# Embedding bags on one core: twenty features counted and twelve gathered, with gathers that wait on TensorE's count

## The chip, the cores and the metric

The kernel runs on one core of a Trainium2 chip. The metric is the device time of one execution in microseconds (us), taken as the median of several runs. The program uses all five engines: TensorE (PE in the rows, PEld for its weight loads), VectorE (DVE), ScalarE (ACT), GpSimd (POOL) and SyncE (SP), the last of which only issues DMAs here. A trailing q (SPq) means an engine's sequencer.

## The reference, cut to what matters

There are 512 samples, 32 features, up to 20 lookups a bag, tables of 12500 rows and 64 numbers a row. A bag's result is the sum of the first `length` rows that its ids name.

```python
flat = tables.reshape(F_ * V_, E_)
offs = jnp.arange(F_, dtype=ids.dtype)[None, :, None] * V_
emb = flat[ids + offs]
mask = (jnp.arange(L_) < lengths[..., None]).astype(emb.dtype)
pooled = jnp.einsum('bfle,bfl->bfe', emb, mask)
out = pooled.reshape(Bq, F_ * E_)
return jnp.nan_to_num(out)
```

## The kernel before, in words

The features are split in two kinds, which are worked on side by side.

**Counted features** (the first M = 22). For such a feature the whole table is loaded, and TensorE multiplies it by a matrix that says how often each bag names each row. The order is written out by hand. A feature has two halves of 256 samples, each of 7 chunks, which makes 14 *stages* a feature, numbered 0 to 13 here. In a stage VectorE makes the one-hot operands: one `onehot_p` (L740) and six `onehot_j` (L742). TensorE multiplies these into `pairs` (L515, in `count`), three evictions a stage. One more eviction stands at the head of each half (`single`, L726 and L728), so a feature has 44. ScalarE copies each from PSUM into `counts` (L470, in `save_counts`). Between the pairs TensorE multiplies the counts of the half before by the table (`sums`, L525). The semaphore `counted` rises by one with each eviction that TensorE has written. VectorE may begin stage s once stage s-2 has been counted (`AHEAD = 2`), so it can run almost two stages ahead of TensorE. In stages 6, 9 and 12 VectorE also splits a piece of the table into bfloat16 parts (`cut_rest` L751, `cut_low` L759). In stages 1 and 8 it reads the sums (L778), and in stage 10 it cleans the result (`clean_pooled`). SP loads the next table chunk in stages 0 to 6 and stores the feature before in stage 11.

**Gathered features** (the other 10). Their 5120 bags are sorted by length and cut into 40 *tiles* of 128 bags. A tile's rows are fetched with one indirect DMA a lookup (L427, in `gather`): lookup l of 128 bags at once, as many as its longest bag has. GpSimd issues them. There are 8 buffers, so the tiles run in 5 *bodies* of 8. In each body deep and shallow tiles take turns (`sorted_tile`). VectorE adds a tile's rows with one reduction (L800, in `add_rows`) and cleans four tiles after every fourth. GpSimd then puts these four with four indirect DMAs (L437, in `put`). After an add, SP clears the buffer with zeros (L346) and loads the next records (L350). The adds stand at the end of stages 0, 4 and 13 of even features and 3 and 11 of odd ones, from feature 2, stage 13 on (`ADDS`, `FIRST_ADD`).

The gather of lookup l waits for the landing of the last gather but one of its tile. So at most two gathers of a tile are in flight. TensorE's and GpSimd's programs are loops; VectorE's, ScalarE's and SP's are written out in full. Feature 0 also holds the preparation: VectorE sorts the lengths and works out the columns of the lookups between its first stages (`prepare`).

Of the kernel before, what the change touches and what calls it, by code (L numbers as in the profile page):

```python
# [22 lines left out]

P = 128
M = 22
TRIO = 3
GROUP = 2 * TRIO
SETS = 2
# [11 lines left out]
def turn(l):  # L40
    return l % 2
# [5 lines left out]

PARTED_BY_VECTOR = {6: 1, 9: 3, 12: 6}

ADDS = (0, 4, 13), (3, 11)  # L50
FIRST_ADD = 2, 8
READ_FIRST, READ_SECOND, CLEAN = 1, CHUNKS + 1, CHUNKS + 3

SKIP = 1 << 22
# [8 lines left out]
ALU = mybir.AluOpType  # L63
# [6 lines left out]
I32 = mybir.dt.int32  # L70
# [11 lines left out]
def build_embedding_bag(nc, ids, lengths, tables, lookup_ids, lookup_lengths, lookup_place, ramps, triangle,  # L82
                        out_counted, out_gathered):
    B, F, L = ids.shape
    _, V, E = tables.shape
    J, HALF, GROUPS = geometry(B, V)
    G = F - M
    BLOCKS = B // P
    TILES = BLOCKS * G
# [5 lines left out]
    CE = JC * E  # L95
    HALVES = M * 2
    N = HALVES * GROUPS
# [6 lines left out]
    BODIES = TILES // BUFFERS  # L104
    STAGES = 2 * CHUNKS
# [10 lines left out]
    STORES = 2 * TRIO + LAST_WORDS  # L116


    added_at = {}
    for f in range(M):  # L120
        for stage in ADDS[f % 2]:
            if (f, stage) >= FIRST_ADD and len(added_at) < TILES:
                added_at[f, stage] = len(added_at)
    LEFT = len(added_at)

    with ExitStack() as ctx:
        def sb(name, shape, dt):
            return ctx.enter_context(nc.sbuf_tensor(name, shape, dt))
# [31 lines left out]
        place_now = sb("place_now", [P, BUFFERS], I32)  # L160
        rank = sb("rank", [P, TILES], I32)
        depth = sb("depth", [P, TILES], I32)

        arrived, arrival = (sb(name, [P, 2, TILES], I32) for name in ("arrived", "arrival"))
        is_nan = sb("is_nan", [P, max(BLOCKS, SLOTS) * E], U8)

        FIRST_HALVES = slice(0, 2)
# [31 lines left out]
        rank_f, depth_f = piece(TILES, F32), piece(TILES, F32)  # L199

        runs_f = until[:, 4 * TILES:(4 + L // 4) * TILES].rearrange("p (t q) -> p t q", t=TILES)
        turn_f, arrival_f = (until[:, 2 * x * TILES:2 * (x + 1) * TILES].rearrange("p (x t) -> p x t", x=2) for x in range(2))
# [28 lines left out]
        counted = sem("counted")  # L231
# [17 lines left out]
        rows_in = [[sem(f"rows_in{k}_{x}") for x in range(2)] for k in range(BUFFERS)]  # L249
# [55 lines left out]
        def column(t):  # L305
            return t % BUFFERS * BODIES + t // BUFFERS
# [7 lines left out]
        def _(sp):  # L314
# [54 lines left out]

            for f in range(1, M):  # L370
                for stage in range(STAGES):
# [11 lines left out]
        @block.gpsimd  # L383
        def _(pool):
            for out, pattern, base, by in (
                (value, [[1, L + 1]], 0, 0),
                (first_row, [[V, G], [0, L]], M * V, 0),
                (position, [[0, G], [1, L]], 0, 0),
                (records[:, :, L], [[P, TILES]], 0, 1),
                (lane[:], [[1, 1]], 0, 1),  # L390
            ) + tuple(
                (last_rank[:, column(k):column(k) + BODIES],
                 [[(sorted_tile(k + BUFFERS) - sorted_tile(k)) * P, BODIES]], sorted_tile(k) * P + P - 1, 0)
                for k in range(BUFFERS)
            ):
                nc.gpsimd.iota(out, pattern=pattern, base=base, channel_multiplier=by).then_inc(iotas_done, 1)
            last_row = pool.to_reg(F * V - 1)

            for k in range(BLOCKS):
                pool.wait_ge(records_ready, k + 1)  # L400
                for t in range(k * G, (k + 1) * G):
                    nc.gpsimd.indirect_dma_start(  # L402
                        out=sorted_records, out_offset=bass.IndirectOffsetOnAxis(ap=rank[:, t:t + 1], axis=0),
                        in_=records[:, t, :], in_offset=None).then_inc(records_out, 16)
            pool.wait_ge(records_out, 16 * TILES)
            for t in range(BUFFERS):
                s = sorted_tile(t)
                nc.gpsimd.dma_start(row_now[:, t, :], sorted_records[s * P:(s + 1) * P, :]).then_inc(first_records_in, 16)
            pool.wait_ge(depths_ready, 1)
            pool.wait_ge(first_records_in, 16 * BUFFERS)  # L410

            def gather(b, k):

                pool.wait_ge(buffer_ready[k], b * 32 + 16)
                pool.sem_inc(fill_begun, 1)
                n = pool.value_load(depth[0:1, bass.ds(b + column(k), 1)], min_val=2, max_val=L)
                landed = [pool.value_load(arrived[0:1, x, bass.ds(b + column(k), 1)], min_val=0, max_val=16 * L * BODIES)
                          for x in range(2)]
                with ExitStack() as deeper:
                    for l in range(L):  # L420
                        if l > 1:
                            deeper.enter_context(pool.If(n > l))
                        x = turn(l)
                        if l > 1:
                            pool.wait_ge(rows_in[k][x], landed[x] + 16 * sum(turn(i) == x for i in range(l)))
                            pool.sem_inc(fill_begun, 1)
                        nc.gpsimd.indirect_dma_start(  # L427
                            out=rows[:, k, l * E:(l + 1) * E], out_offset=None, in_=table_rows,
                            in_offset=bass.IndirectOffsetOnAxis(ap=row_now[:, k, l:l + 1], axis=0),
                            bounds_check=last_row, oob_is_err=False).then_inc(rows_in[k][x], 16)  # L430

            def put(b, x):

                pool.wait_ge(gathered_ready, b * 2 + (x + 1))
                pool.sem_inc(fill_begun, 1)
                for k in range(x * SLOTS, (x + 1) * SLOTS):
                    nc.gpsimd.indirect_dma_start(  # L437
                        out=out_gathered, out_offset=bass.IndirectOffsetOnAxis(ap=place_now[:, k:k + 1], axis=0),
                        in_=gathered[:, k * E:(k + 1) * E], in_offset=None).then_inc(gathered_stored[x], 16)

            def body(b, first):
                for k in range(BUFFERS):
                    if not first and k % SLOTS == PUT_AT:
                        put(b - 1, k // SLOTS)
                    gather(b, k)

            body(0, True)
            with pool.Fori(1, BODIES) as b:
                body(b, False)
            for x in range(2):  # L450
                put(BODIES - 1, x)
                pool.wait_ge(gathered_stored[x], 16 * SLOTS * BODIES)
# [148 lines left out]
        def _(dve):  # L601
            done = [0]

            def step(ins):
                done[0] += 1
                ins.then_inc(prepared, 1)
                dve.wait_ge(prepared, done[0])
# [42 lines left out]
            def find_depths():  # L650

                fits = has[:, 0:TILES * L].rearrange("p (t l) -> p t l", l=L)
                step(nc.vector.tensor_tensor(fits, below[:, 1:L + 1].unsqueeze(1).to_broadcast([P, TILES, L]),
                                             last_rank.unsqueeze(2).to_broadcast([P, TILES, L]), ALU.is_le))
                step(nc.vector.tensor_reduce(out=depth_f, in_=fits, axis=AX_X, op=ALU.add))
                step(nc.vector.tensor_reduce(out=runs_f, in_=fits.rearrange("p t (q x) -> p t q x", x=4)[:, :, :, 1::2],
                                             axis=AX_X, op=ALU.add))
                step(nc.vector.tensor_reduce(out=turn_f[:, 1, :], in_=runs_f, axis=AX_X, op=ALU.add))
                step(nc.vector.tensor_scalar(depth_f, depth_f, 2.0, None, ALU.max))
                step(nc.vector.tensor_scalar(turn_f[:, 1, :], turn_f[:, 1, :], 1.0, None, ALU.max))  # L660
                step(nc.vector.tensor_copy(depth[:], depth_f))
                step(nc.vector.tensor_tensor(turn_f[:, 0, :], depth_f, turn_f[:, 1, :], ALU.subtract))
                for k in range(BUFFERS):
                    mine = slice(column(k), column(k) + BODIES)
                    for x in range(2):
                        nc.vector.tensor_tensor_scan(arrival_f[:, x, mine], turn_f[:, x, mine], turn_f[:, x, mine], 0.0,
                                                     ALU.add, ALU.max).then_inc(scanned, 1)
                dve.wait_ge(scanned, 2 * BUFFERS)
                step(nc.vector.tensor_tensor(turn_f, arrival_f, turn_f, ALU.subtract))
                step(nc.vector.tensor_scalar(arrived[:], turn_f, 16.0, None, ALU.mult))  # L670
                step(nc.vector.tensor_scalar(arrival[:], arrival_f, 16.0, None, ALU.mult))
                dve.sem_inc(depths_ready, 1)

# [226 lines left out]
```

## Time and profile before

| what | us |
|---|---|
| median of 3 runs | 1185.06 |
| lowest and highest run | 1184.69, 1189.72 |
| span of the profiled execution | 1287.7 |
| TensorE busy in it | 1118.5 |
| VectorE busy in it | 992.5 |
| GpSimd busy in it | 547.5 |

The profiled execution is 102.6 us longer than the median of the runs shown. Its span is from the first to the last instruction; no separate total of it is given. Feature f begins for VectorE at 9.2, 92.6, 143.7 us and so on; features 16 to 21 begin at 960.1, 1012.8, 1060.1, 1109.8, 1158.7 and 1207.8 us. The last gather is issued at 958.2 us and the last add at 1074.7 us, so features 19 and 20 hold counted work alone.

### The profile page before, as it was taken

What the parts mean: (1) busy time and instruction counts of PE and PEld (TensorE: products, weight loads), DVE (VectorE), ACT (ScalarE), POOL (GpSimd) and SP (SyncE); (2) the same over time, 40 slices, a digit from 0 to 9 for tenths busy, and PEclk for the clock granted to TensorE, in tenths of its full rate; (3) what the DMA queues carried; (4) which work ended last, traced back from release to release, by engine and by line L of the source; (5) the groups of instructions that cost most, each with busy time, mean ns of one, the idle gap of its engine ahead of it and who ended that gap; (6) DMA issues with size and microseconds to landing.
All of it is one profiled execution on the core that took longest, in us unless ns stands there. A gap on an engine that the chain in (4) does not pass through costs nothing.

```text
span 1287.7 us, 31751 instructions
## 1 busy us (share of the span) xinstructions
PE 1118.5 (87%) x10873; PEld 969.4 (75%) x10873; DVE 992.5 (77%) x2692; ACT 827.6 (64%) x1233; POOL 547.5 (43%) x519
## 2 busy tenths in 40 slices
PE   3379999896988878989979888979789999999996
PEld 1168888785876767778868767868678888888886
DVE  9657788884886867869868867969678898787881
ACT  4257787673756656757747566757557777787780
POOL 4865665556555455555565544555540101000000
PEclk9989999897999988999989989989989999999998
DMA  5324234241433333242414333242413213123120
GB/s 184 116 68 115 60 83 144 74 136 45 135 107 95 117 86 97 81 132 82 143 46 136 106 95 118 82 130 69 134 25 100 58 55 104 47 62 100 35 73 5
DMA packets 63916, 118.38 MB, mean 92 GB/s; under 512 B 30120, under 2 KB 31742, under 8 KB 63840
## 3 DMA queue, kind: packets, MB, share of 16 engines
q1 hardware_dynamic: 46608, 102.19, 25.5%
q0 software_dynamic: 16032, 15.00, 5.9%
q10 hardware_dynamic: 1200, 0.50, 0.2%
q14 instruction: 68, 0.56, 0.1%
q8 instruction: 8, 0.13, 0.0%
HBM read 87.19 MB, written 4.62 MB: 71 GB/s over the span
## 4 chain that ended last, share of the span: by engine, by line
PE 73%; DVE 10%; another core or an unknown queue 7%; ACT 7%; issue 3%; DVEq 0%; POOL 0%; POOLq 0%
PE sums L525 48%; PE pairs L515 19%; PE rest L543 6%; DVE onehot_j L742 3%; ACT counts L470 3%; ACT table L482 2%; DVE gathered L800 1%; DVE onehot_p L740 1%; ACT rest L478 1%; DVE table L751 1%; ACT table L486 0%; DVE table L759 0%; DVEq L796 0%; DVE is_nan L768 0%
## 5 line engine op out<-in xcount | busy, mean ns | idle before, releaser
L525 PE MATMUL sums<-table,counts 128*128 128x192 bf16 x8624 | 909.0, 251 | 0.8 <-issue 0.8
L470 ACT ACTIVATE counts<-pairs 128x588 int16<-128x588 f32 (+1 forms) x968 | 617.0, 650 | 368.9 <-PE pairs L515 262.7
L525 PEld LDWEIGHTS sums<-table,counts 128*128 128x128 fp8e3 x8624 | 776.3, 98 | 55.0 <-issue 0.4
L427 POOL DMA_INDIRECT rows<-tables,row_now x413 | 453.3, 1098 | 376.7 <-issue 206.1
L742 DVE TENSOR_SCALAR onehot_j<-ramp,j_of,worth 128x296 bf16<-128x296 f16 x1848 | 536.3, 353 | 0.0
L515 PE MATMUL pairs<-onehot_j,onehot_p 128*128 128x294 bf16 x1892 | 410.4, 297 | 112.8 <-ACT counts L470 67.3
L740 DVE TENSOR_TENSOR onehot_p<-ramp,p_of 128x768 bf16<-128x768 f16 x308 | 169.9, 552 | 253.7 <-PE pairs L515 172.9
L515 PEld LDWEIGHTS pairs<-onehot_j,onehot_p 128*128 128x128 bf16 x1892 | 178.2, 98 | 187.3 <-issue 107.8
L543 PE MATMUL rest<-table,minus_eye 128*128 128x448 bf16 x352 | 102.5, 373 | 38.2 <-ACT table L482 17.1
L486 ACT ACTIVATE table<-rest 128x896 f32<-128x896 f32 x88 | 80.8, 918 | 35.3 <-remote 23.6
L437 POOL DMA_INDIRECT out_gathered<-gathered,place_now x40 | 42.4, 1061 | 132.3 <-DVE gathered L771 121.0
L482 ACT ACTIVATE table<-rest 128x896 f32<-128x896 f32 x88 | 80.8, 918 | 26.1 <-remote 9.8
L800 DVE TENSOR_REDUCE gathered<-rows 128x64 f32<-128x1280 f32 x40 | 94.3, 2356 | 0.0
L478 ACT ACTIVATE rest<-table 128x896 f32<-128x896 f32 x88 | 80.7, 917 | 0.0
L751 DVE TENSOR_TENSOR table<-table 128x896 f32<-128x896 f32 x66 | 71.5, 1083 | 0.0
L759 DVE TENSOR_TENSOR table<-table 128x896 f32<-128x896 f32 x66 | 69.5, 1053 | 0.0
L543 PEld LDWEIGHTS rest<-table,minus_eye 128*128 128x128 bf16 x352 | 24.2, 98 | 58.4 <-ACT table L482 25.6
L402 POOL DMA_INDIRECT sorted_records<-records,rank x40 | 45.6, 1139 | 26.3 <-DVE records L617 14.4
L778 DVE TENSOR_REDUCE pooled<-sums 128x128 f32<-128x384 f32 x44 | 23.8, 542 | 21.3 <-PE sums L525 20.5
L728 DVE TENSOR_SCALAR onehot_j<-ramp,j_of,worth 128x296 bf16<-128x296 f16 x44 | 17.3, 392 | 0.0
L726 DVE TENSOR_SCALAR onehot_p<-ramp,p_of 128x128 bf16<-128x128 f16 x44 | 12.8, 291 | 0.0
L771 DVE COPY_PREDICATED pooled<-is_nan,zeros 128x256 f32<-128x256 uint8 x22 | 10.0, 453 | 0.8
(68 smaller groups left out, 79.8 us busy)
## 6 DMA issues: line engine op xcount, KB each, us to landing
table<-tables SPq DMA_DIRECT2D x154, 448.0 KB
rows<-zeros SPq DMA_DIRECT2D x40, 640.0 KB
rows<-tables,row_now POOLq DMA_INDIRECT x413
out_counted<-pooled SPq DMA_DIRECT2D x132, 21.0 KB
rows<-lookup_ids SPq DMA_DIRECT2D x1, 903.0 KB, 8.5
rows<-lookup_lengths SPq DMA_DIRECT2D x1, 903.0 KB, 10.2
out_counted<-pooled SPq DMA_DIRECT2D x44, 1.0 KB
sorted_records<-records,rank POOLq DMA_INDIRECT x40
```

The lines of the kernel that those rows point to most:

```text
L427: nc.gpsimd.indirect_dma_start(out=rows[:, k, l * E:(l + 1) * E], out_offset=None, in_=table_rows, in_offset=bass.IndirectOffsetOnAxis(ap= ...
L470: nc.scalar.activation(dst, src, ACT.Copy).then_inc(counts_saved, 1)
L478: nc.scalar.activation(rest[:, :, 0:CE // 2], both_halves(0, c), ACT.Copy).then_inc(chunk_copied, 1)
L482: nc.scalar.activation(both_halves(1, c), rest[:, :, 0:CE // 2], ACT.Copy).then_inc(middle_ready, 1)
L486: nc.scalar.activation(both_halves(2, c), rest[:, :, 0:CE // 2], ACT.Copy).then_inc(low_saved, 1)
L515: last = nc.tensor.matmul(pair(h, c, q)[:, x, 0:WIDE], onehot_p[:, s, k, :, side], onehot_j[:, s, i + 1, 0:WIDE], start=True, stop=True)
L525: last = nc.tensor.matmul(sums[h][:, k * PARTS * E:(k + 1) * PARTS * E], counts[h][:, j, :, k], parts[:, :, j, :, 1], start=(j == 0 and k ...
L543: last = nc.tensor.matmul(rest[:, x, 0:CE // 2], minus_eye[:], upper_halves(part)[:, half], start=False, stop=True, skip_group_check=True)
L740: nc.vector.tensor_tensor(onehot_p[:, s, 1:, :, :], ramp_twice.unsqueeze(1).to_broadcast([P, PAIRS, P, 2]), of_chunk.unsqueeze(2).to_broad ...
L742: nc.vector.tensor_scalar(onehot_j[:, s, i + 1, :], ramp[:, 2 * P:], j_of[:, n:n + 1], worth[:, 0:1], ALU.is_equal, ALU.mult).then_inc(one ...
L751: nc.vector.tensor_tensor(table[:, 1, sl], table[:, 0, sl], upper_halves(0)[:, sl], ALU.subtract).then_inc(rest_done, 1)
L800: nc.vector.tensor_reduce(out=gathered[:, k * E:(k + 1) * E], in_=rows[:, k, :].rearrange("p (l e) -> p e l", e=E), axis=AX_X, op=ALU.add)
```

## The change

M goes from 22 to 20. So two features fewer are counted, and twelve are gathered: 48 tiles in 6 bodies in place of 40 in 5. The adds stand at stage number 41 + 5t for tile t (number 14 f + stage of the whole run), which is feature 2, stage 13 for the first and feature 19, stage 10 for the last. The gathers no longer wait for landings. Before lookups 0, 2, 4, ... GpSimd waits until `counted` has reached a value that depends on the tile and the lookup: 72 evictions for the first tile, 31 more for each pair of tiles, 125 more for each body, 7 more for each five lookups. An odd tile begins later by an amount from its depth (`later`, one more VectorE instruction in the preparation), and `arrived` goes, with two VectorE instructions.

```diff
-M = 22
+M = 20
...
-ADDS = (0, 4, 13), (3, 11)
-FIRST_ADD = 2, 8
+FIRST_ADD = 41
+ADD_EVERY = 5
+FIRST_GATHER = 72
+PAIR_OF_TILES = 31
+PER_BODY = 125
+
+def since(l):
+    return 7 * l // 5
...
+    added_at = {divmod(FIRST_ADD + ADD_EVERY * t, STAGES): t for t in range(TILES)}
...
-                landed = [pool.value_load(arrived[0:1, x, bass.ds(b + column(k), 1)], min_val=0, max_val=16 * L * BODIES)
-                          for x in range(2)]
+                start = b * PER_BODY + (FIRST_GATHER + PAIR_OF_TILES * (k // 2))
+                if k % 2:
+                    start = start + pool.value_load(later[0:1, bass.ds(b + column(k), 1)], min_val=0, max_val=PAIR_OF_TILES)
...
-                        x = turn(l)
-                        if l > 1:
-                            pool.wait_ge(rows_in[k][x], landed[x] + 16 * sum(turn(i) == x for i in range(l)))
+                        if l % 2 == 0:
+                            pool.wait_ge(counted, start + since(l))
                             pool.sem_inc(fill_begun, 1)
...
+                nc.vector.tensor_scalar(later[:], depth_f, -1.4, PAIR_OF_TILES - 2.0, ALU.mult, ALU.add)
...
-                step(nc.vector.tensor_tensor(turn_f, arrival_f, turn_f, ALU.subtract))
-                step(nc.vector.tensor_scalar(arrived[:], turn_f, 16.0, None, ALU.mult))
```

On GpSimd, in the first gathers of the first tile, before:

```order
L427 DMA rows<-tables,row_now 128x64 x2
L422 COMPARE_AND_BRANCH
L425 REGISTER_ALU
L427 DMA rows<-tables,row_now 128x64 [waits rows_in0_0]
L422 COMPARE_AND_BRANCH
L425 REGISTER_ALU
L427 DMA rows<-tables,row_now 128x64 [waits rows_in0_1]
```

On GpSimd, the head of the second tile (an odd one), after:

```order
L421 TENSOR_LOAD depth [waits buffer_ready1]
L421 ISA x2
L424 TENSOR_LOAD later
L424 ISA x2
L430 REGISTER_ALU
L432 DMA rows<-tables,row_now 128x64 [waits counted]
L432 DMA rows<-tables,row_now 128x64
L428 COMPARE_AND_BRANCH
L430 REGISTER_ALU
L432 DMA rows<-tables,row_now 128x64 [waits counted]
L428 COMPARE_AND_BRANCH
L432 DMA rows<-tables,row_now 128x64
```

Each gather from the third on waited for a landing (`rows_in`). Now each second gather waits for TensorE's count, the first of a tile too, and the one behind it waits for nothing.

On VectorE, from stage 12 of feature 6 on, before:

```order
L740 TENSOR_TENSOR onehot_p<-ramp,p_of 128x768
L742 TENSOR_SCALAR onehot_j<-ramp,j_of,worth 128x296 x2
L751 TENSOR_TENSOR table<-table 128x896
L742 TENSOR_SCALAR onehot_j<-ramp,j_of,worth 128x296 x3
L759 TENSOR_TENSOR table<-table 128x896
L742 TENSOR_SCALAR onehot_j<-ramp,j_of,worth 128x296
L740 TENSOR_TENSOR onehot_p<-ramp,p_of 128x768
L742 TENSOR_SCALAR onehot_j<-ramp,j_of,worth 128x296 x6
```

The same place on VectorE, from the second cut of the table on, after:

```order
L763 TENSOR_TENSOR table<-table 128x896
L746 TENSOR_SCALAR onehot_j<-ramp,j_of,worth 128x296
L800 TENSOR_LOAD arrival
L800 ISA x2
L800 TENSOR_LOAD arrival
L800 ISA x2
L804 TENSOR_REDUCE gathered<-rows 128x64
L807 COPY place_now<-row_now 128x1
L772 TENSOR_TENSOR is_nan<-gathered 128x256
L773 TENSOR_SCALAR gathered<-gathered 128x256
L775 COPY_PREDICATED gathered<-is_nan,zeros 128x256
L744 TENSOR_TENSOR onehot_p<-ramp,p_of 128x768
```

An add with its cleaning now stands behind the cuts of stage 12, ahead of the one-hots of stage 13. Before, no add stood in a stage that has cuts.

## Rows read from the trace of the kernel before

**Rows 1.** The page: span, and each engine's busy time.

```profile
span 1287.7 us, 31751 instructions
PE 1118.5 (87%) x10873; PEld 969.4 (75%) x10873; DVE 992.5 (77%) x2692; ACT 827.6 (64%) x1233; POOL 547.5 (43%) x519
```

**Rows 2.** The page's 40 slices: GpSimd busy, granted TensorE clock, both in tenths.

```profile
POOL 4865665556555455555565544555540101000000
PEclk9989999897999988999989989989989999999998
```

**Rows 3.** The page: shares of the chain of work that ended last.

```profile
PE 73%; DVE 10%; another core or an unknown queue 7%; ACT 7%; issue 3%; DVEq 0%; POOL 0%; POOLq 0%
```

**Rows 4.** Stretches: start:end length, each engine's busy us (instructions), clock, DMA.

```profile
0.00:92.60 92.60, 44.75 (x266) 27.01 (x267) 66.69 (x184) 36.76 (x54) 57.23 (x71) 0.94 0.37 127
92.60:143.70 51.10, 48.74 (x497) 43.17 (x496) 39.22 (x116) 37.65 (x57) 28.90 (x25) 1.00 0.31 82
92.60:960.10 867.50, 761.70 (x7409) 663.35 (x7408) 672.09 (x1802) 562.52 (x841) 481.33 (x440) 0.95 0.35 99
960.10:1109.80 149.70, 146.25 (x1489) 129.60 (x1487) 134.77 (x363) 113.12 (x169) 8.94 (x8) 1.00 0.24 69
1109.80:1158.70 48.90, 48.32 (x496) 43.10 (x494) 38.91 (x115) 37.55 (x57) 0.00 (x0) 1.00 0.25 69
1158.70:1207.80 49.10, 48.48 (x497) 43.21 (x496) 39.02 (x116) 37.71 (x57) 0.00 (x0) 1.00 0.23 68
1207.80:1287.70 79.90, 68.95 (x730) 63.13 (x727) 41.02 (x119) 39.91 (x60) 0.00 (x0) 0.95 0.15 44
```

**Rows 5.** Groups in feature 19 (1109.8 to 1158.7): busy, mean ns, idle before.

```profile
L525 PE MATMUL sums<-table,counts 128*128 128x192 bf16 x394 | 40.8, 247 | 0.0
L740 DVE TENSOR_TENSOR onehot_p<-ramp,p_of 128x768 bf16<-128x768 f16 x14 | 7.8, 555 | 9.9 <-PE pairs L515 9.9
```

**Rows 6.** Timeline of VectorE, an add in stage 13: start, length, engine, line.

```profile
1008.91 2.37 DVE L800 TENSOR_REDUCE gathered<-rows 128x64 f32<-128x1280 f32 x1
1011.37 0.42 DVE L768 TENSOR_TENSOR is_nan<-gathered 128x256 uint8<-128x256 f32 x1
...
1012.38 0.30 DVE L726 TENSOR_SCALAR onehot_p<-ramp,p_of 128x128 bf16<-128x128 f16 x1
```

**Rows 7.** Timelines: the first stage of all, then stages 12 and 13 of feature 19.

```profile
9.23 0.55 DVE L740 TENSOR_TENSOR onehot_p<-ramp,p_of 128x768 bf16<-128x768 f16 x1
10.93 0.66 ACT L470 ACTIVATE counts<-pairs 128x588 int16<-128x588 f32 x1 [0.76 <-PE pairs L515]
...
1156.19 0.54 DVE L740 TENSOR_TENSOR onehot_p<-ramp,p_of 128x768 bf16<-128x768 f16 x1
1159.50 0.67 ACT L470 ACTIVATE counts<-pairs 128x588 int16<-128x588 f32 x1 [0.42 <-PE pairs L515]
```

**Rows 8.** Line L427, all gathers: shortest, median and longest in ns.

```profile
L427 POOL DMA_INDIRECT rows<-tables,row_now x413: 991/1000/2072, 84.3 to 958.2; - x138
```

**Rows 9.** Timeline around 296 us, all engines; idle time before in brackets.

```profile
294.89 1.03 POOL L437 DMA_INDIRECT out_gathered<-gathered,place_now  x1 [0.30 <-issue]
295.42 1.39 SPq L342 DMA_DIRECT2D out_counted<-pooled  x2
...
304.39 0.66 ACT L470 ACTIVATE counts<-pairs 128x588 int16<-128x588 f32 x1 [8.97 <-remote]
```

**Rows 10.** Timelines of VectorE and GpSimd in the preparation.

```profile
12.66 1.03 DVE L645 TENSOR_TENSOR counts<-counts 128x840 f32<-128x840 f32 x1
...
44.78 0.96 POOL L402 DMA_INDIRECT sorted_records<-records,rank  x1 [0.30 <-issue]
...
47.99 2.03 DVE L681 SCALAR_TENSOR_TENSOR rows<-rows 128x1806 f32<-128x1806 f32 x1
...
48.50 2.84 POOL L402 DMA_INDIRECT sorted_records<-records,rank  x1 [0.30 <-issue]
```

More of the change, by code:

```diff
@@ L116, in build_embedding_bag @@
     STORES = 2 * TRIO + LAST_WORDS
[L119 to L124, printed above, removed]
+    added_at = {divmod(FIRST_ADD + ADD_EVERY * t, STAGES): t for t in range(TILES)}
+    assert FIRST_ADD + ADD_EVERY * (TILES - 1) < M * STAGES
+    LEFT = TILES
     with ExitStack() as ctx:
@@ L162, in build_embedding_bag @@
         depth = sb("depth", [P, TILES], I32)
-        arrived, arrival = (sb(name, [P, 2, TILES], I32) for name in ("arrived", "arrival"))
+        later = sb("later", [P, TILES], I32)
+        arrival = sb("arrival", [P, 2, TILES], I32)
         is_nan = sb("is_nan", [P, max(BLOCKS, SLOTS) * E], U8)
@@ L429, in gather @@
                             in_offset=bass.IndirectOffsetOnAxis(ap=row_now[:, k, l:l + 1], axis=0),
-                            bounds_check=last_row, oob_is_err=False).then_inc(rows_in[k][x], 16)
+                            bounds_check=last_row, oob_is_err=False).then_inc(rows_in[k][turn(l)], 16)
             def put(b, x):
```

## Prediction

> **What bounds the kernel now.** I read the page's busy times and slices first, then the chain of waits, then a table of stretches cut at the features, and last the timelines of single stages. TensorE is busiest, with 1118.5 of 1287.7 us, ahead of VectorE with 992.5 [rows 1], and it holds 73% of the chain that ended last [rows 3]. Averages hide what matters, so look at the stretches. Features 19 and 20 hold counted work alone. They take 48.9 and 49.1 us, and TensorE is busy for 48.3 and 48.5 us of that [rows 4]. A feature without gathers is TensorE's own work and nothing else; I take 49.0 us. In such a feature VectorE idles 9.9 us, all of it in waits for TensorE ahead of a stage's one-hots [rows 5]. This idle time is what the adds of gathered tiles live on.
>
> Features 1 to 15 have gathers, and in the profiled execution they take 867.5 us, or 57.8 us each [rows 4]. The clock is granted at 0.95 there and dips below full in several slices; GpSimd works through just these slices [rows 2, 4]. Now set this against the timed runs. The stretches at both ends are 92.6 us and 149.7 + 48.9 + 49.1 + 79.9 = 327.6 us [rows 4]. If the timed run matches the profile there, the fifteen features have 1185.06 - 92.6 - 327.6 = 764.9 us, or 51.0 us each. So the 102.6 us by which the profile exceeds the median lie almost wholly in the gather features. They come as single stalls: at 295.4 us, beside a put and a store, ScalarE stops for 8.97 us and the rest stops behind it [rows 9]. I treat such stalls as mostly the profiled execution's own and work against the median, keeping them as a rival.
>
> **The change part by part.**
>
> *Two counted features fewer.* They leave from the steady part: 2 x 49.0 = -98.0 us. Nothing hides this, as TensorE is the bound there [rows 4].
>
> *Preparation.* VectorE sorts 48 tiles in place of 40, so its instructions over all tiles grow by a fifth; one of 840 numbers takes 1.03 us [rows 10]. About ten of that size come to 10 x 0.2 = +2 us. The long ones over all lookups, such as that of 2.03 us [rows 10], shrink by a tenth, about -0.8 us. Two small instructions go and one comes. GpSimd sends 8 more tiles of sorted records at 0.96 + 0.30 = 1.26 us [rows 10], 10 us more. These are hidden: the gathers now begin at eviction 72, which is 28 evictions of 49.0 / 44 = 1.11 us behind 92.6 us, about 124 us, against 84.3 before [rows 8]. Sum: between 0 and +4, taken as +1.5 us.
>
> *The adds.* One add is 2.37 us, and every fourth has about 1.1 us of cleaning behind it: from 1008.91 to 1012.38 it is 3.47 us [rows 6]. Eight more come. What do they cost TensorE? Features 16 to 18 hold 7 adds and no gathers, and take 149.7 us where three bare features take 147.0: 2.7 us, or 0.39 us an add [rows 4]. Eight more at that rate are +3 us. Their new places cost more. VectorE begins stage 13's one-hots at 1156.19, and ScalarE takes the first eviction of that stage at 1159.50, a lead of 3.31 us; in the very first stage, where nothing is ahead, the same distance is 1.70 us [rows 7]. So the slack is 1.6 us. An add in stage 12 (3 of the 48, and two of these with cleaning) overdraws it by 2.37 - 1.6 = 0.8 or 3.47 - 1.6 = 1.9 us, together 4.6 us. Before, no add stood there. A walk through the other stages in the same way finds about 3 us more, in stages behind an add in stage 6 or 10 or with cleaning in stage 11, and 1 us that the old places cost. So the places add about +7 us, and all adds together +10. The bounds are +3 (the measured rate alone) and +22 (every add late by 0.8 us, 48 x 0.8 - 40 x 0.39).
>
> *More gathers.* 413 gathers for 40 tiles [rows 8] make about 496 for 48. Their cost to TensorE without adds shows in feature 1: 51.1 us against 49.0 with 25 of them [rows 4], 0.08 us each. By the median it is 764.9 - 15 x 49.0 = 30 us, less 13 us for the 33 adds there, over 408 gathers: 0.04 us each. 83 more at 0.06 are +5 us; bounds +3 and +7.
>
> *The new waits on TensorE's count.* Behind GpSimd's wait stand its own later gathers and the puts, and nobody else. The tile is waited for by VectorE's add. Tile 0 begins at eviction 72 and is issued by about 98, in stage number 31; its add stands at 41. Both advance by 10 stages a pair (31 evictions of 22/7 a stage are 9.9), so some nine stages of 3.5 us, 31 us, stay between them to the end. Is GpSimd fast enough? A pair has 413 / 40 x 2 = 20.7 gathers of 1.00 + 0.30 us [rows 8, 10], 26.9 us; two puts, 2.6 us; and two tile heads, about 2 us: 31.5 us. The pace is 31 evictions of about 51.7 / 44 = 1.17 us, 36.4 us. It keeps up, so the wait itself costs nothing. That gathers come evenly and never in bursts may also give something back: from 0 down to the whole price of gathers, 496 x 0.04 = -20 us. I take 0, as feature 1 paid its 2.1 us with gathers that were paced by landings. SP's new order, refills at other stages, costs nothing: it waits for an add that VectorE makes about a stage ahead of TensorE.
>
> *A rule that speaks against it.* While VectorE ran the 2.03 us instruction in the preparation, a GpSimd DMA that otherwise took 0.96 us took 2.84 us [rows 10]. The Trainium skill's page SBUF — State Buffer, section Who interferes with whom, has a VectorE instruction in a 2-port mode and GpSimd block each other fully. The row agrees. By that rule gathers could lengthen with more VectorE work; but the median gather is 1.00 us beside 49-us features full of VectorE work [rows 8], so the sum leaves it out and the slow rival below takes it up.
>
> **Sum.** 1185.06 - 98.0 + 1.5 + 10 + 5 = 1103.6; I say 1103 us. As a check by stretches: 94.1 for the head, 49.7 for feature 1, 17 features of 51.0 + 0.6, and 81 for the last, are 1102 us.
>
> **The rivals.**
>
> *Even pacing pays.* The gather features lose most of their extra: 1103 less 9 to 20 us, 1083 to 1094. For it: the bursts of puts, stores and gathers at the stall [rows 9]. Against it: puts and stores remain as they are.
>
> *VectorE becomes the bound.* The adds cost their upper bound, +22 in place of +10, perhaps a little more: 1113 to 1130. For it: VectorE's idle 9.9 us [rows 5] against 2.8 adds of 2.37 + 0.3 = 7.5 us a feature, unevenly placed.
>
> *The wait is empty.* If GpSimd is always late, `counted` has passed each value when it comes, and gathers run back to back as before but without landing waits. Nothing waits for them, so the time is the sum's, 1103 to 1110.
>
> *Stalls of the profiled kind stand in timed runs too.* Then a share of 9 us [rows 9] at each of 12 puts, say a third to two thirds of 108 us, comes on top: 1135 to 1175.
>
> *GpSimd falls behind and VectorE waits for rows (slower).* At x us a gather a pair takes 20.7x + 4.6 us against 36.4. The 31 us of slack are used up over 24 pairs once x is 1.6. Beyond, each pair adds its excess, and the run is slower than before when 24 (20.7x - 31.8) - 31 passes 82 us, at x = 1.76. With 1.8 us it is 1103 + 24 x 5.5 - 31 = 1204 us. Against it: the median is 1.30 with issue, and the longest of all is 2.07 [rows 8].
>
> **How the numbers follow.** Forecast (1094 to 1113) 0.46; pacing pays 0.22; VectorE the bound 0.18; wait empty 0.07; stalls 0.05; GpSimd behind 0.02. The range 1086 to 1124 takes the forecast, the empty wait and most of the two neighbours. A measurement of this kernel can tell about 0.5%, 6 us. Only the last case is slower and none lies near no change: faster 0.97, same 0.01, slower 0.02.
>
> **What would show it.** In the profile after: bare features of 49.0 us at its start only, since gathers reach feature 18; GpSimd's idle time before L432 released by TensorE in place of landings, in pairs of gathers about 3.3 us apart; in feature 6, stage 13 late by some 2 us behind the add of stage 12; a sum of adds of 48 x 2.37. Idle VectorE ahead of the adds' reduction would mean that GpSimd is behind. If gather features run near 49 us, the landing waits' bursts were the cost. I am wrong below 1086 if the extra of the gather features was not the adds' and gathers' at all, and above 1124 if the stalls belong to the timed runs.

## The result, and the profile after

The kernel after takes 1047.36 us (median of 4 runs, 1046.27 to 1047.80) against 1187.39 us for the kernel before in the same comparison (1184.69 to 1192.81). The ratio is 0.881, with a 95% interval of 0.878 to 0.885. The gain is 140 us where I had forecast 82, and the time lies 39 us below the range.

The page of the kernel after, in the lines that answer to [rows 1 to 3]:

```profile
span 1045.4 us, 29010 instructions
PE 983.3 (94%) x9885; PEld 864.1 (83%) x9885; DVE 937.4 (90%) x2485; ACT 754.1 (72%) x1121; POOL 666.0 (64%) x617
...
POOL 3874677676676756777667767767676775773010
PEclk9999999999999999999999999999999999999998
...
PE 79%; DVE 16%; ACT 2%; issue 1%; DVEq 1%; POOL 0%; POOLq 0%
```

The span is 2.0 us under the time of the same execution (1047.35 us). TensorE is busy for 94% of it in place of 87%, and its clock is granted at nine tenths or more in every slice but the last. Now the stretches, with the columns of [rows 4]: the head, feature 1, features 1 to 18, and the last feature with the tail.

```profile
0.00:74.20 74.20, 40.86 (x266) 25.10 (x266) 67.09 (x183) 36.26 (x54) 46.43 (x57) 1.00 0.43 154
74.20:123.20 49.00, 48.42 (x497) 43.17 (x496) 39.30 (x115) 37.64 (x57) 24.93 (x28) 1.00 0.30 79
74.20:965.10 890.90, 873.97 (x8904) 776.70 (x8902) 821.38 (x2176) 678.12 (x1010) 614.93 (x557) 1.00 0.41 118
965.10:1045.40 80.30, 68.50 (x721) 62.29 (x719) 48.90 (x128) 39.68 (x59) 4.66 (x4) 0.96 0.16 45
```

Eighteen features take 890.9 us, or 49.5 us each, although all but a part of the first have gathers. Feature 1 takes 49.0 us, as long as a bare one, although the first gathers fall into it. The head takes 74.2 us where [rows 4] had 92.6. The gathers themselves, as [rows 8]:

```profile
L432 POOL DMA_INDIRECT rows<-tables,row_now x495: 991/1004/2057, 108.3 to 946.6; - x165
```

And from the list of waits (total, number and longest, in us):

```profile
POOL rows L432 <- PE pairs L520: 128.9, 137, 14.6
POOL rows L432 <- issue: 116.7, 358, 1.3
...
DVE gathered L804 <- issue: 3.5, 4, 0.9
```

GpSimd waits for TensorE's count, as the change says, and VectorE hardly ever waits ahead of an add's reduction.

### The profile page after: what moved, and what is told of

It reads as the page before. It is cut to its first block, busy times and chain, and to the rows that moved or that the text cites. A ratio compares the mean times of both kernels' runs of the same rounds, so it can differ in the third digit from the quotient of the medians.

```text
span 1045.4 us, 29010 instructions
## 1 busy us (share of the span) xinstructions
PE 983.3 (94%) x9885; PEld 864.1 (83%) x9885; DVE 937.4 (90%) x2485; ACT 754.1 (72%) x1121; POOL 666.0 (64%) x617
## 4 chain that ended last, share of the span: by engine, by line
PE 79%; DVE 16%; ACT 2%; issue 1%; DVEq 1%; POOL 0%; POOLq 0%
PE sums L530 55%; PE pairs L520 18%; PE rest L548 6%; DVE onehot_j L746 5%; DVE gathered L804 3%; DVE onehot_p L744 2%; ACT table L487 1%; DVE table L755 1%; DVE table L763 1%; ACT counts L475 1%; DVEq L800 1%; DVE is_nan L772 0%; DVE gathered L775 0%; DVE counts L636 0%; DVE j_of L688 0%
## 5 line engine op out<-in xcount | busy, mean ns | idle before, releaser
L530 PE MATMUL sums<-table,counts 128*128 128x192 bf16 x7840 | 806.7, 247 | 0.0
L475 ACT ACTIVATE counts<-pairs 128x588 int16<-128x588 f32 (+1 forms) x880 | 563.7, 651 | 239.5 <-PE pairs L520 232.8
L530 PEld LDWEIGHTS sums<-table,counts 128*128 128x128 fp8e3 x7840 | 690.1, 96 | 44.4 <-issue 0.2
L432 POOL DMA_INDIRECT rows<-tables,row_now x495 | 553.3, 1118 | 245.6 <-PE pairs L520 128.9
L746 DVE TENSOR_SCALAR onehot_j<-ramp,j_of,worth 128x296 bf16<-128x296 f16 x1680 | 491.9, 355 | 0.0
L520 PE MATMUL pairs<-onehot_j,onehot_p 128*128 128x294 bf16 x1720 | 364.6, 292 | 40.6 <-DVE onehot_j L746 28.3
L520 PEld LDWEIGHTS pairs<-onehot_j,onehot_p 128*128 128x128 bf16 x1720 | 159.5, 97 | 101.0 <-issue 27.9
L744 DVE TENSOR_TENSOR onehot_p<-ramp,p_of 128x768 bf16<-128x768 f16 x280 | 153.7, 549 | 72.7 <-PE pairs L520 71.9
L804 DVE TENSOR_REDUCE gathered<-rows 128x64 f32<-128x1280 f32 x48 | 114.3, 2381 | 3.5 <-issue 3.5
L442 POOL DMA_INDIRECT out_gathered<-gathered,place_now x48 | 52.4, 1091 | 69.3 <-issue 67.1
L487 ACT ACTIVATE table<-rest 128x896 f32<-128x896 f32 x80 | 73.4, 918 | 13.9 <-PE rest L548 6.2
L491 ACT ACTIVATE table<-rest 128x896 f32<-128x896 f32 x80 | 73.4, 918 | 8.2 <-PE rest L548 0.5
L732 DVE TENSOR_SCALAR onehot_j<-ramp,j_of,worth 128x296 bf16<-128x296 f16 x40 | 16.1, 402 | 0.0
```

The lines of the kernel that those rows point to most:

```text
L432: nc.gpsimd.indirect_dma_start(out=rows[:, k, l * E:(l + 1) * E], out_offset=None, in_=table_rows, in_offset=bass.IndirectOffsetOnAxis(ap= ...
L475: nc.scalar.activation(dst, src, ACT.Copy).then_inc(counts_saved, 1)
L487: nc.scalar.activation(both_halves(1, c), rest[:, :, 0:CE // 2], ACT.Copy).then_inc(middle_ready, 1)
L491: nc.scalar.activation(both_halves(2, c), rest[:, :, 0:CE // 2], ACT.Copy).then_inc(low_saved, 1)
L520: last = nc.tensor.matmul(pair(h, c, q)[:, x, 0:WIDE], onehot_p[:, s, k, :, side], onehot_j[:, s, i + 1, 0:WIDE], start=True, stop=True)
L530: last = nc.tensor.matmul(sums[h][:, k * PARTS * E:(k + 1) * PARTS * E], counts[h][:, j, :, k], parts[:, :, j, :, 1], start=(j == 0 and k ...
```

## The experiments

Theory A, formed on this result: with waits on landings GpSimd needs more time for a tile than the adds leave it, so VectorE waits ahead of its adds, and TensorE behind it. I took this wait for one for the rows; the first experiment shows that it mostly was for something else that GpSimd does. The rivals were B, that the places of the adds had gained the time, or that the stalls belonged to one execution; and C, that the even pacing of the gathers spared the other engines. Each ratio is to the kernel before as it was measured beside that run; its medians were 1186.36 to 1188.70 us there, so differences from it are good to a few us.

### The kernel before, profiled again

No edit.

> The kernel before, unchanged, to see whether its stalls are a property of the kernel or of one execution. Theory A (the landing waits stall the core in every execution): about 1187 us, with the stalls of 5 to 9 us in features 4 to 15 in the trace again. Theory B (the stalls of the trace of before belong to that one execution, whose span was 100 us over the median): 1187 us by the clock of the runs, with a trace near 1185 us, feature 0 near 64 us as in the kernel after, and gather features of 51 to 52 us without single stalls.

Measured: 1190.63 us (10 runs), ratio to the kernel before 1.002 (0.998 to 1.005). The new trace spans 1191.2 us, within 1 us of its median, and it differs from the one that I had read. Here are its stretches (head, features 1 to 17, rest):

```profile
0.00:73.50 73.50, 40.70 (x266) 25.06 (x267) 66.51 (x185) 36.36 (x54) 46.83 (x57) 1.00 0.44 156
73.50:965.10 891.60, 834.73 (x8408) 740.34 (x8406) 762.16 (x2042) 639.88 (x953) 489.26 (x457) 0.97 0.37 104
965.10:1191.20 226.10, 213.42 (x2204) 191.92 (x2202) 163.39 (x468) 152.40 (x227) 7.68 (x7) 0.99 0.21 61
```

From its list of waits, VectorE's ahead of the reduction:

```profile
DVE gathered L800 <- issue: 57.6, 5, 24.6
```

And the reduction's row among the groups of the trace that I had read:

```profile
L800 DVE TENSOR_REDUCE gathered<-rows 128x64 f32<-128x1280 f32 x40 | 94.3, 2356 | 0.0
```

The last number is the idle time before the reduction: 0.0 us then, 57.6 us now, in five waits. The profile puts them down to "issue", which says only that it shows nothing that was waited for on the way there. What ended them stands in the view of the puts (line L437), under "who waited for it (us, times)":

```profile
  DVE gathered L800: 57.6, 5
```

All of it is a wait for puts. An add waits for more than its rows, which the description of the kernel before leaves out. From `add_rows`, cut:

```python
                if b and k % SLOTS == 0:

                    dve.wait_ge(gathered_stored[k // SLOTS], 16 * SLOTS * b)
```

The first add of each four writes where the puts of four earlier tiles read, so it waits until they have landed. And GpSimd issues these puts late: in `body` they stand behind the gathers of the first two tiles of the four (`k % SLOTS == PUT_AT`, with `PUT_AT = 2`). The five waits are those of tiles 16, 20, 24, 32 and 36. The longest is a picture of the mechanism. The timeline of VectorE around it:

```profile
638.00 1.68 DVE L742 TENSOR_SCALAR onehot_j<-ramp,j_of,worth 128x296 bf16<-128x296 f16 x6
664.27 2.30 DVE L800 TENSOR_REDUCE gathered<-rows 128x64 f32<-128x1280 f32 x1 [24.59 <-issue]
```

GpSimd meanwhile:

```profile
639.33 1.04 POOL L427 DMA_INDIRECT rows<-tables,row_now  x1 [2.45 <-DMA rows<-tables,row_now]
640.67 1.00 POOL L427 DMA_INDIRECT rows<-tables,row_now  x1 [0.31 <-issue]
642.90 1.00 POOL L427 DMA_INDIRECT rows<-tables,row_now  x1 [1.23 <-DMA rows<-tables,row_now]
644.34 0.99 POOL L427 DMA_INDIRECT rows<-tables,row_now  x1 [0.45 <-issue]
647.36 0.99 POOL L427 DMA_INDIRECT rows<-tables,row_now  x1 [2.03 <-issue]
...
655.27 0.99 POOL L427 DMA_INDIRECT rows<-tables,row_now  x1 [0.47 <-issue]
656.58 1.03 POOL L437 DMA_INDIRECT out_gathered<-gathered,place_now  x1 [0.30 <-issue]
...
660.45 0.96 POOL L437 DMA_INDIRECT out_gathered<-gathered,place_now  x1 [0.30 <-issue]
661.71 1.03 POOL L427 DMA_INDIRECT rows<-tables,row_now  x1 [0.30 <-issue]
```

VectorE stands for 24.6 us at the add of tile 24, while GpSimd is still issuing the gathers of the next tile, two by two, each pair held up by a landing. Only behind these come the four puts, and the add begins 2.9 us after the last of them. Neither theory was right about this run as written: the stalls of 5 to 9 us of [rows 9] are gone (B), but waits of up to 25 us stand in their place, and they are the kernel's own (A). The first trace was of an execution about 100 us longer than the others, with stalls even ahead of its first gather at 84.3 us: VectorE stood for 7.5 us before 76.26 us, and the profile names no engine of the core that it waited for ("remote"). GpSimd's own pace was the same in both traces, 873.9 us from the first gather to the last then and 876.0 us now. The stalls of the other engines gave it the time, so that VectorE never had to wait ahead of a reduction.

### The kernel after with landing waits

```diff
-                        if l % 2 == 0:
-                            pool.wait_ge(counted, start + since(l))
+                        x = turn(l)
+                        if l > 1:
+                            pool.wait_ge(rows_in[k][x], landed[x] + 16 * sum(turn(i) == x for i in range(l)))
```

`arrived` and its two instructions come back with it, and `later` goes.

> The kernel after (20 counted features, even adds) with the old waits on landings put back, nothing else. Theory A (the landing waits are what cost time beyond the two features): 1047 + 17 gather features x 2.5 to 3 us = 1090 to 1100 us. Theory B (the places of the adds, and with them the refills by SP, were the cost): 1047 to 1052 us.

Measured: 1199.67 us (10 runs), 1.011 (1.007 to 1.014) of the kernel before. So with two counted features fewer, and without the new waits, the kernel is 1% slower than before. The waits were worth 152 us there, three times what I expected of theory A. VectorE's idle time ahead of the reductions is about as long, in the row of that group:

```profile
L804 DVE TENSOR_REDUCE gathered<-rows 128x64 f32<-128x1280 f32 x48 | 113.7, 2370 | 149.9 <-issue 149.2 <-DMA rows<-tables,row_now 0.7
```

In the view of the puts (L441), "who waited for it" has nearly all of this:

```profile
  DVE gathered L804: 145.7, 10
```

The gathers (shortest, median and longest in ns, first and last start in us):

```profile
L431 POOL DMA_INDIRECT rows<-tables,row_now x495: 992/1000/2063, 100.4 to 1134.2; - x165
```

### The kernel before with count waits

```diff
-                            pool.wait_ge(rows_in[k][x], landed[x] + 16 * sum(turn(i) == x for i in range(l)))
+                            pool.wait_ge(counted, start + since(l))
```

With `FIRST_GATHER = 72`, `PAIR_OF_TILES = 35` and `PER_BODY = 141`, for even l only and with `later`, as after.

> The kernel before (22 counted features, the old places of the adds) with the gathers waiting on TensorE's count, at 35 evictions a pair and 141 a body since the old adds are 5.6 stages apart. Theory A (landing waits): the whole extra of the gather features goes, 1187 - 15 x 2.5 to 3 = about 1143 us. Theory B (places of the adds): 1185 us.

Measured: 1136.34 us (1135.38 to 1136.78), ratio 0.956 (0.951 to 0.962). The waits alone give 51 to 54 us (against the median of the kernel before and of its repeat), where the trace of the repeat showed VectorE waiting 57.6 us; theory A had put the time 7 us higher. Theory B falls here, as the adds stood where they had been. The idle time ahead of the reduction is 0.0 us:

```profile
L807 DVE TENSOR_REDUCE gathered<-rows 128x64 f32<-128x1280 f32 x40 | 95.2, 2380 | 0.0
```

### The kernel before with even adds

```diff
-    for f in range(M):
-        for stage in ADDS[f % 2]:
-            if (f, stage) >= FIRST_ADD and len(added_at) < TILES:
-                added_at[f, stage] = len(added_at)
+    added_at = {divmod(41 + 5 * t, STAGES): t for t in range(TILES)}
```

> The kernel before with the adds every five stages from stage number 41 on, landing waits kept. Theory A (landing waits): 1187 + 0 to 7 us, since the new places cost VectorE's lead behind cut stages. Theory B (places of the adds): about 1145 us.

Measured: 1254.85 us, ratio 1.055 (1.049 to 1.062), 66 us slower than before. Both expectations missed, and the miss sharpened theory A. The even adds leave GpSimd 5 stages, 17.5 us, for a tile; the old ones left 5.6 stages, 19.6 us. With landing waits it needs more than either, by the gathers' first and last start:

```profile
L423 POOL DMA_INDIRECT rows<-tables,row_now x413: 991/999/2041, 85.4 to 955.0; - x138
```

And VectorE's wait ahead of the reduction, of which 108.5 us were for puts:

```profile
DVE gathered L796 <- issue: 111.1, 10, 21.7
```

From the first gather to the last it is (955.0 - 85.4) / 40 = 21.7 us a tile.

### The kernel after with 22 counted features

```diff
-M = 20
+M = 22
```

> The kernel after with 22 counted features and 10 gathered in place of 20 and 12, so 40 tiles in place of 48; count waits and even adds stay. It prices the two features alone. Theory A (landing waits made GpSimd late, nothing else beyond the features): 1047 + 2 x 49.0 less 8 adds at 0.2 to 0.4 us = 1143 us, and within 8 us of the 1136 us of the old adds with count waits. Theory B (the even adds or the even pacing give something of their own): well below 1136 us.

Measured: 1142.68 us (1142.10 to 1143.40). That is what theory A expected. So two counted features more, with eight tiles fewer, cost 95.3 us, and the even adds cost 1142.68 - 1136.34 = 6.3 us over the old places.

### The kernel after with no waits ahead of gathers

```diff
-                        if l % 2 == 0:
-                            pool.wait_ge(counted, start + since(l))
```

> The kernel after with no wait at all ahead of a gather but that for its buffer: neither landings nor counts. Theory A (GpSimd's rate with landing waits was the bound; any way of waiting less serves): 1047 to 1050 us, no idle VectorE ahead of an add, some 16 us a tile on GpSimd. Theory C (gathers in bursts harm the other engines, and the even pacing by the count is what gains): 1047 plus 10 to 40 us, with stalls of ScalarE or late table loads beside bursts of gathers.

Measured: 1046.56 us (1045.61 to 1047.11), ratio to the kernel before 0.881 (0.876 to 0.887), which is the kernel after's own. Theory C falls: gathers that run as early as their buffers allow, one behind the other, cost no time here. The pacing gives nothing; what gained was that the landing waits went.

### One gather in flight

```diff
-                        x = turn(l)
-                        if l > 1:
+                        x = turn(l - 1)
+                        if l > 0:
                             pool.wait_ge(rows_in[k][x], landed[x] + 16 * sum(turn(i) == x for i in range(l)))
```

This is an edit of the kernel after with landing waits.

> The kernel after with landing waits made stricter: each gather waits for the one just before it, so one is in flight in place of two. A dose of the suspected cause. Theory A (GpSimd's rate sets the time by the landings): a landing takes about 3.5 to 4 us from issue by the pairs in the trace of the kernel before, so a tile takes about 40 us in place of 21 and the run about 86 + 48 x 40 = 2000 us. Theory C (the harm is contention by gathers in flight): fewer in flight, so below the 1200 us of two in flight.

Measured: 1913.21 us (a single run, with its profile), 87 us under what I had worked out: a tile took 36.8 us in place of 40. A stricter wait costs more, as theory A says and against C. GpSimd's waits:

```profile
POOL rows L431 <- DMA rows<-tables,row_now: 1047.9, 426, 4.3
```

And the gathers:

```profile
L431 POOL DMA_INDIRECT rows<-tables,row_now x495: 991/995/2121, 100.8 to 1865.5; - x165
```

### Fourteen features gathered

```diff
-M = 20
+M = 18
-FIRST_ADD = 41
-ADD_EVERY = 5
+FIRST_ADD = 28
+ADD_EVERY = 4
```

This is an edit of the kernel with no waits ahead of gathers.

> Two more features gathered: 18 counted, 14 gathered (56 tiles), adds every four stages from stage number 28, and no waits ahead of gathers. TensorE's bare work falls by 98 us to about 950. Theory A: a tile takes GpSimd some 16 us against the 14 us of four stages, so GpSimd is the bound again: 86 + 56 x 15.7 = 965 us to the last gather, and 1000 to 1035 us in all. If VectorE is the bound (39.5 + 3.1 x 2.7 = 48 us of each 49 us feature, unevenly placed): 960 to 990 us.

Measured: 1055.69 us (1054.57 to 1056.45), 21 us over the upper end and slower than the kernel after. GpSimd is the bound again, now by its own work. The gathers:

```profile
L426 POOL DMA_INDIRECT rows<-tables,row_now x581: 992/1000/2036, 112.1 to 989.8; - x194
```

VectorE's waits ahead of the reduction; of the first line 69.7 us were for puts, and the second were for rows:

```profile
DVE gathered L798 <- issue: 74.1, 17, 11.4
DVE gathered L798 <- DMA rows<-tables,row_now: 18.8, 4, 13.3
```

That is 877.7 / 56 = 15.7 us a tile, as by the count of the prediction (31.5 us a pair), against 14.0 us for four stages. What I had missed is the start, at 112 us. The 86 us were those of kernels with 40 tiles, and with 48 the run with landing waits had begun at 100.4; sixteen tiles more to sort and send come first here.

### Adds where VectorE has lead

```diff
-    added_at = {divmod(FIRST_ADD + ADD_EVERY * t, STAGES): t for t in range(TILES)}
+    added_at = {(3 + t // 3, (0, 4, 8)[t % 3]): t for t in range(TILES)}
```

This too is an edit of the kernel with no waits ahead of gathers.

> No waits ahead of gathers as in the run without waits, and the adds in stages 0, 4 and 8 of features 3 to 18, where by the walk through VectorE's lead none delays TensorE. Theory A: the 8 to 9 us by which the gather features of the kernel after exceed 49.0 us are the adds behind the cuts of stages 6, 9 and 12 and behind the cleaning of stage 10; they go, and the time is 1047 - 9 = 1038 us. Rival: what is left beyond 49.0 us comes from the gathers in flight (0.02 us each), and the time stays at 1045 to 1047 us. If a tile takes GpSimd more than the 4.67 stages (16.4 us) that are left for it, VectorE waits for rows and it is over 1050 us.

Measured: 1037.30 us (6 runs, 1036.80 to 1037.81), ratio to the kernel before 0.874 (0.871 to 0.877): 9 to 10 us below both the kernel after and the one without waits, and the fastest of all. Features 1 to 18 and the last with the tail:

```profile
73.80:955.10 881.30, 870.54 (x8890) 775.97 (x8888) 824.12 (x2180) 677.89 (x1008) 608.30 (x562) 1.00 0.41 119
955.10:1035.70 80.60, 69.68 (x737) 63.80 (x735) 42.62 (x125) 40.28 (x60) 0.00 (x0) 0.96 0.16 43
```

Eighteen features now take 881.3 us, 48.96 us each. With 48 adds and 495 gathers beside them they are as short as bare ones [rows 4].

### What the runs say together

| kernel | GpSimd us a tile | left by the adds | VectorE waited ahead of reductions | of that, for puts | longer than its twin without landing waits |
|---|---|---|---|---|---|
| before, repeated (22, two in flight) | 21.9 | 19.6 | 57.6 | 57.6 | 54.3 |
| even adds (22, two in flight) | 21.7 | 17.5 | 111.1 | 108.5 | 112.2 |
| after with landing waits (20, two in flight) | 21.5 | 17.5 | 149.9 | 145.7 | 152.3 |
| the same, one in flight | 36.8 | 17.5 | 851.3 | 541.3 | 865.9 |
| fourteen gathered (18, no waits) | 15.7 | 14.0 | 92.9 | 69.7 | none run |

The first column is the time from the first gather to the last over the number of tiles. The twins are the count-wait kernel with the old adds (1136.34), the one with 22 features (1142.68), and the kernel after (1047.36) for the other two. The third and the last column agree within 4 us for two in flight, and within 2% for one: the landing waits act through VectorE's wait for GpSimd, and for little else that these runs show. TensorE's clock had a small part at most: with landing waits on 20 features it was granted at 0.939 over the span in place of 0.997, in slices behind VectorE's waits at six to eight tenths, and TensorE was busy for 1004.5 us in place of 983.3, but the whole run was only 2.4 us longer than the waits explain.

What VectorE waited for was GpSimd's puts, more than its rows. Would it have waited without them? An estimate: in the run with landing waits the last add began at 1155.4 us after 149.9 us of waits, so without them at 1005.5. The last gather was issued at 1134.2 us, and a gather lands 2.5 us after its issue by the median of that trace. So at least 131 us of wait would have been left for rows alone; by the same working it is 42 of the 57.6 us in the repeat. GpSimd's rate is thus the main cause, and the place of the puts, behind two more tiles of gathers, adds the rest. No run moved the puts or gave `gathered` more room, so this split is not shown by a run.

The 140.0 us of the change come apart into three steps that were each run: waits on the count in place of landings, 1187.4 to 1136.3, -51.1; even adds, 1136.3 to 1142.7, +6.3; two features counted fewer and gathered, 1142.7 to 1047.4, -95.3. The first step is 52.4 us against the kernel before as measured beside that run (1188.70). The order matters. Made first, the even adds cost 66 us, and with them in place the waits give 112 us, and 152 us at 20 features.

## Why the prediction was wrong, point by point

The sum gave 1103.6 us, 56.2 us too much. Of this 51.1 us are the term of the new waits, taken as 0; 6.8 us are the two features with their gathers; the rest is the places of the adds and the median of the kernel before, 1187.39 in the comparison in place of 1185.06.

**Two counted features fewer, -98.0 us: right; more gathers, +5: mis-sized.** The step with 22 and 20 features measured -95.3 us. With the gathers' +5, the preparation's +1.5 and the eight adds at the measured rate (+3) I had -88.5. The preparation was near: the head takes 74.2 us in place of the repeat's 73.5. The gathers cost nothing that can be seen in features 1 to 18 of the fastest kernel. The 2.1 us of feature 1 in [rows 4] belonged to the long execution; the same feature takes 49.0 us in the trace of the repeat and of the kernel after.

**The places of the adds, +7: right.** The even adds cost 6.3 us, and moving them to stages 0, 4 and 8 took 9 to 10 us off. The walk had put 1.9 us behind the add with cleaning in stage 12 of feature 6. In the trace of the kernel after stage 13 of that feature has its one-hots right behind the cleaning, with no idle time ahead of them, and TensorE stands 1.81 us for them:

```profile
366.73 2.40 DVE L804 TENSOR_REDUCE gathered<-rows 128x64 f32<-128x1280 f32 x1
369.06 0.14 DVE L807 COPY place_now<-row_now 128x1 int32<-128x1 int32 x1
369.23 0.43 DVE L772 TENSOR_TENSOR is_nan<-gathered 128x256 uint8<-128x256 f32 x1
369.57 0.53 DVE L773 TENSOR_SCALAR gathered<-gathered 128x256 f32<-128x256 f32 x1
370.14 0.45 DVE L775 COPY_PREDICATED gathered<-is_nan,zeros 128x256 f32<-128x256 uint8 x1
370.48 0.55 DVE L744 TENSOR_TENSOR onehot_p<-ramp,p_of 128x768 bf16<-128x768 f16 x1
...
371.53 0.42 PE L520 MATMUL pairs<-onehot_j,onehot_p 128*128 128x294 bf16 x2 [1.81 <-DVE onehot_j L746]
```

**The new waits, 0: this is the step that failed.** I asked whether GpSimd would be fast enough after the change, found 31.5 us a pair against 36.4, and was right; the run with 18 features measured just that, 15.7 us a tile. But I never put the same question to the kernel before. [Rows 8] held the answer: 413 gathers from 84.3 to 958.2 us are 21.8 us a tile, and the adds of the kernel before stand 5.6 stages of 3.5 us apart, 19.6 us. GpSimd was behind, and taking its waits away had to give something: 51.1 us. The list of who waits for GpSimd was incomplete too. I wrote that behind its wait stand its later gathers and the puts, "and nobody else"; but VectorE's first add of each four waits for the puts, and that is where it stood, 57.6 of 57.6 us in the repeat. My slow rival had the mechanism in the main (GpSimd behind, VectorE waiting for it) and put it after the change, where it stood before it.

**The base from which the extra of the gather features was taken: wrong with it.** I divided 764.9 us among fifteen features on the premise that the timed runs matched the profile at both ends. They did not: the head is 73.5 us in the repeat, not 92.6. And I took what was left of the extra (30 us) for a price of gathers and adds, which the kernel after would pay too. In truth most of it was VectorE's waits for GpSimd. The sum so kept in the time after what the change took away. A span 102.6 us over the median was a warning that I used to explain the stalls away, when it should also have made me distrust that trace's zeros: its VectorE never waited ahead of a reduction, since the long stalls had given GpSimd the time.

**The rivals.** "Even pacing pays" came closest by its number, and its mechanism is refuted: with no pacing at all the time is the same. "VectorE becomes the bound" did not come, though VectorE is busy for 90% of the span. "The wait is empty" is half true, in that the wait is not needed. Stalls of the profiled kind stood in no other trace of this study; what made that one execution long is open, as no run repeated it. Whether a limit of more than two in flight would do as well as none was not tried. The rule that I had taken from the Trainium skill's page SBUF — State Buffer, section Who interferes with whom, that VectorE and GpSimd can block each other, changed nothing for the gathers: their median is 1.00 us, within 1%, in all kernels, beside a VectorE that is up to 90% busy.

**The row behind that rule: read too simply.** The DMA of 2.84 us began beside the 2.03 us instruction [rows 10], but that one ended at 50.02 us and the DMA at 51.34. The next VectorE instruction ended 0.12 us before the DMA did:

```profile
50.06 1.16 DVE L683 TENSOR_SCALAR rows<-rows,place 128x1806 f32<-128x1806 f32 x1
```

So the row does not show which of the two held the DMA up, nor in what mode either ran.

## What to carry to other kernels

Before pricing what an engine off the bound will need after a change, divide what it does now by what its consumers leave it now; a producer that is 10% too slow hides in a profile, because its waits show up rarely and as idle time of another engine. Then list all that the consumer waits for, not its data alone: here it was the buffer that the slow engine had still to empty. Where the profile puts a wait down to "issue", the view of each candidate line says who waited for it. A wait that only limits how many transfers are in flight sets a rate, near latency over number in flight (3.6 us a gather with one and 2.1 with two here), and it belongs into the same sum as the issue time. When a profiled span is 9% over the median, take medians of single instructions from it and no waits, and no absence of waits either.

## What the runs showed of the hardware that was not expected

- GpSimd's gathers of 128 rows by 256 bytes need no spacing at all here. With none it issued one each 1.3 us (median 1.00 busy and 0.30 of issue), with up to twenty of a tile unawaited, and TensorE was no slower for it: features of 48.96 us, most of them beside some 32 gathers each.
- The landing is long against the issue, 2.5 us from the issue by the median against 1.0 us of busy time. With one in flight a gather took (1865.5 - 100.8) / 495 = 3.6 us, tile heads and puts included, with two 2.1 us, and with no limit 15.7 x 56 / 581 = 1.5 us.
- One execution of an unchanged kernel on one core can stall in many places (ten waits of VectorE ahead of its one-hots, 70.4 us, that the profile puts down to no engine of the core; the repeat has none) and last 1287.7 us where the others lasted 1181.5 to 1197.8; the kernels without landing waits varied by 2 us or less over 4 to 6 runs.
